# Five one-input VectorE operations of an image stage, written with a tile of ones as second input

## The reference

```python
def _layernorm(x, axis=-1, eps=1e-05):
    m = jnp.mean(x, axis=axis, keepdims=True)
    v = jnp.var(x, axis=axis, keepdims=True)
    return (x - m) / jnp.sqrt(v + eps)
...
        sig = jax.nn.sigmoid(logits)
        choice = sig + e_bias[None, :]
...
        topk_idx = jax.lax.top_k(scores_for_choice, K)[1]
        topk_w = jnp.take_along_axis(sig, topk_idx, axis=1)
        topk_w = topk_w / (topk_w.sum(-1, keepdims=True) + 1e-20)
        topk_w = topk_w * SCALE
```

## Time and profile before

| what | value |
|---|---|
| median of 3 runs | 4340.14 us (4337.72 to 4344.22) |
| span of the profiled execution | 4339.1 us; its page gives no time of its own beside the span |
| instructions | 74496 |
| TensorE matmul, weight load | 3835.0 us (88%), 2899.2 us (67%) |
| VectorE | 3261.9 us (75%), 5523 instructions |
| ScalarE | 2637.8 us (61%), 4838 instructions |
| GpSimd | 3020.4 us (70%), 1609 instructions |
| mean granted TensorE clock | 0.968 of full speed |

### The profile page before, as it was taken

The page is one execution under the profiler, slowest core; times in us unless marked ns, Lnnn a source line. Parts: engine busy times, 40 slices in busy tenths (PEclk is TensorE's granted clock), DMA queues, the critical chain, the costliest instruction groups (busy, mean ns, idle before and its releaser), DMA issues. The chain is left out here.

```text
span 4339.1 us, 74496 instructions
## 1 busy us (share of the span) xinstructions
PE 3835.0 (88%) x22114; PEld 2899.2 (67%) x22114; DVE 3261.9 (75%) x5523; ACT 2637.8 (61%) x4838; POOL 3020.4 (70%) x1609
## 2 busy tenths in 40 slices
PE   3469999999999999999999999988879999999997
PEld 2346666666676666766666666656558888888886
DVE  1788888888889888898888988887246666666663
ACT  1468877888778888788887788875522222222221
POOL 0888888878788787887888878886025555555554
PEclk8669999999999999999999999999989999999999
DMA  3333333333333333333333333321057777777775
GB/s 81 86 85 82 93 90 91 99 83 89 94 84 92 92 84 94 88 94 96 82 90 94 92 89 92 89 71 53 16 127 183 186 184 185 184 183 185 184 186 115
DMA packets 243533, 473.54 MB, mean 109 GB/s; under 512 B 39644, under 2 KB 162080, under 8 KB 243220
## 3 DMA queue, kind: packets, MB, share of 16 engines
q1 hardware_dynamic: 203792, 429.90, 37.4%
q0 software_dynamic: 36864, 37.98, 5.6%
q10 hardware_dynamic: 2564, 1.82, 0.2%
HBM read 404.99 MB, written 64.56 MB: 108 GB/s over the span
## 5 line engine op out<-in xcount | busy, mean ns | idle before, releaser
L507 POOL TENSOR_TENSOR y<-y,state 128x972 f32<-128x972 f32 x448 | 1016.8, 2270 | 336.0 <-DVE state L668 325.3
L486 POOL TENSOR_TENSOR state<-du,b_rows 128x972 f32<-128x972 f32 x512 | 1187.7, 2333 | 3.0
L662 DVE TENSOR_TENSOR_SCAN ps<-ps,state 128x972 f32<-128x972 f32 x512 | 1113.6, 2181 | 61.1 <-ACT ps L530 47.6
L530 ACT ACTIVATE ps<-delta,a_neg 128x324 f32<-128x324 f32 x1536 | 727.3, 521 | 313.0 <-DVE state L668 250.8
L1040 POOL DMA_INDIRECT out_rows<-yo,scatter_idx x256 | 369.5, 1443 | 426.9 <-DMA out_rows<-yo,scatter_idx 354.0
L668 DVE TENSOR_TENSOR state<-ps,c_rows 128x972 f32<-128x972 f32 x512 | 597.7, 1168 | 35.2 <-DVE ps L662 0.5
L782 PE MATMUL ps<-ws_d,inter 116*98 116x192 f32 (+1 forms) x3072 | 539.2, 329 | 16.3 <-issue 12.9
L782 PEld LDWEIGHTS ps<-ws_d,inter 116*98 116x98 f32 (+1 forms) x3072 | 501.7, 175 | 24.2 <-issue 16.3
L1171 PE MATMUL e_ps<-w_down,e_inter 116*96 116x192 f32 x2048 | 359.9, 329 | 102.1 <-DVE yo L1121 102.1
L754 DVE TENSOR_TENSOR inter<-ag,ps 116x648 f32<-116x648 f32 x256 | 211.5, 826 | 316.9 <-PE ps L767 316.9
L1102 DVE TENSOR_TENSOR e_inter<-e_ag,e_ps 116x384 f32<-116x384 f32 x256 | 139.9, 555 | 375.1 <-ACT e_ag L1066 366.6
(11 more groups left out here) (174 smaller groups left out, 7333.4 us busy)
## 6 DMA issues: line engine op xcount, KB each, us to landing
b_rows<-bc_rows SPq DMA_DIRECT2D x256, 324.0 KB, 5.0
c_rows<-bc_rows SPq DMA_DIRECT2D x256, 324.0 KB, 5.7
w_lo<-in_we_up SPq DMA_DIRECT2D x128, 348.0 KB
w_down<-in_we_down SPq DMA_DIRECT2D x128, 348.0 KB
x_in<-in_x SPq DMA_DIRECT2D x32, 1176.0 KB, 7.7
w_hi<-in_we_up SPq DMA_DIRECT2D x256, 116.0 KB
image_cnt<-running_counts SPq DMA_DIRECT2D x256, 81.0 KB
w_lo<-in_we_up SPq DMA_DIRECT2D x128, 116.0 KB
```

The lines of the kernel that those rows point to most:

```text
L486: nc.gpsimd.tensor_tensor(b.state[n % 4][:], b.du[t.p][:], row, ALU.mult).then_inc(input_ready, 1)
L507: nc.gpsimd.tensor_tensor(y, y, b.state[n % 4][:], ALU.add).then_inc(y_added, 1)
L530: ins = nc.scalar.activation(to[:, c * L:c * L + L], b.delta[t.p][:, c, :], ACT.Exp, scale=b.a_neg[:, c, k:k + 1])
L662: nc.vector.tensor_tensor_scan(s, s, b.state[k % 4][:].rearrange("p a t -> p (a t)"), 0.0, ALU.mult, ALU.add).then_inc(scan_done, 1)
```

## The change

Five `tensor_scalar` calls, each with one tensor input, become `scalar_tensor_tensor` calls. The scalar and its operation stay the first step; the second step is a multiplication by a slice of `ones`. Nothing else is added or moved; semaphores and chains stay.

```diff
@@ ln1_stats, ln2_stats
-                        nc.vector.tensor_scalar(stat[:, m + 1, 4, :], b.mean_var[m][:, :, 1], EPS, None, ALU.add).then_inc(ln_var[m], 1)
+                        nc.vector.scalar_tensor_tensor(stat[:, m + 1, 4, :], b.mean_var[m][:, :, 1], EPS, b.ones[:, 0:6], ALU.add, ALU.mult).then_inc(ln_var[m], 1)
@@ choose
-                            nc.vector.tensor_scalar(b.mask[:], b.ch[:], BIG / 2, None, ALU.is_ge).then_inc(mask_ready, 1)
+                            nc.vector.scalar_tensor_tensor(b.mask[:], b.ch[:], BIG / 2, b.ones[:].unsqueeze(1).broadcast_to([128, 6, E]), ALU.is_ge, ALU.mult).then_inc(mask_ready, 1)
@@ weigh
-                            link(nc.vector.tensor_scalar(den, den, 2e-20, None, ALU.add))
+                            link(nc.vector.scalar_tensor_tensor(den, den, 2e-20, b.ones[:, 0:6], ALU.add, ALU.mult))
                             link(nc.vector.reciprocal(b.top8[:, :, 1], den))
-                            nc.vector.tensor_scalar(b.x2[:, :, :, D], b.top8[:, :, 1].rearrange("p (b k) -> p b k", b=2), SCALE, None, ALU.mult).then_inc(factor_ready, 1)
+                            nc.vector.scalar_tensor_tensor(b.x2[:, :, :, D], b.top8[:, :, 1].rearrange("p (b k) -> p b k", b=2), SCALE, b.ones[:, 0:6].rearrange("p (b k) -> p b k", b=2), ALU.mult, ALU.mult).then_inc(factor_ready, 1)
```

## The result

The changed kernel takes 4,351.7 us (median of 8 runs, 4,344.5 to 4,354.4), the kernel before 4,338.9 (8 runs, 4,335.1 to 4,344.2): a ratio of 1.0023, 95% interval 1.0013 to 1.0033. The medians lie 12.8 us apart, and the interval runs from 5.6 to 14.3 us. It is a small loss, of the forecast's size.

The account below looks back on a forecast made before the run. VectorE's run at the head of a body, reaching TensorE through ScalarE, was taken as the bound. Small instructions 0 plus masks 30 x 0.39 = 11.7 us, on a median of 4,340.1, gave 4,351.8 us; range 4,341 to 4,362.

Parts of the forecast that it names:

- The bound: Head of a body: VectorE's long run reaches TensorE through ScalarE, so a delay there is paid about one to one.
- The small instructions, 0 us: L705, L738, L740, 128 instructions: two-input form held by GpSimd to the same end as before, so 0 us.
- The sign that L705 should keep a mean near 750 ns: L705 after the change: mean stays near 750 ns, since its holds by GpSimd stay.
- The mask, 0.39 us: L728, 768 values per partition: one value per cycle in place of two, 0.39 us longer, held or unheld.
- Passed on one to one, 30 times, 11.7 us: 30 of 32 masks stand where VectorE's run has no gap: each 0.39 us reaches the body, 11.7 us.
- the half-absorbed case: Bodies waiting only at L808: TensorE's own work absorbs the delay there, 5.9 us more, 4,346 us; chance 0.22.
- Nothing is left to absorb: Body at 1557.49: TensorE is already 0.07 us late at L808, so any further VectorE delay counts.
- The last two masks: The two unheld L728 of 560 ns, where VectorE idles behind them: taken to cost 0.
- the delays of the two engines are one: At L728: VectorE's 0.39 us and GpSimd's being kept about 0.39 us longer do not add.
- The freed holds, 22 us: Rival: L705, L738, L740 no longer held by GpSimd; TensorE soon bounds, 22 us saved, 4,318 us; chance 0.06.
- The two races at L717: Rivals at L717 against GpSimd: wins where it loses, 4,325 us, chance 0.06; loses where it wins, 4,383 us, chance 0.04.

Follow-up runs that it names:

- the delay behind the mask: Kernel before plus a VectorE sum over 3 x 102 ones right behind L728, about 0.39 us: ratio 1.0042, 14 to 18 us slower.
- the two runs with a pure delay: Kernel before plus one extra VectorE sum, in one run ahead of L728 (ratio 1.0026), in the other behind it (ratio 1.0042).
- the small ones alone: Kernel before with only L705, L738 and L740 given the second input, the mask L728 left one-input: ratio 0.9995.

## Why the prediction was right, point by point

*The bound.* Right: VectorE's run at the head of a body reaches TensorE through ScalarE. Making it longer by 0.38 us lengthened bodies of both kinds by as much (the delay behind the mask), making it shorter took the waits at L795 and L808 away, and with them gone the mask's extra work was free. One thing is to be added: in the long bodies it is not the wait at L808 that sets the length. Five of them, at a clock of 0.98, have only the 0.46 us there of a load that is not late, and last as long as the others; what all 12 have is the wait at L795.

*The small instructions, 0 us.* Right: 0.9995 alone, and pairs of bodies that agree to 0.01 us. But for one row of 5.05 us, the form that the change brings is held to the same point as the old one. That it would be was readable in a few early rows. The sign that L705 should keep a mean near 750 ns was wrong: it was 855. With the old form beside the new mask it is 807 already; where the rest comes from was not separated.

*The mask, 0.39 us.* 0.40 measured, held and unheld, and it is the whole loss.

*Passed on one to one, 30 times, 11.7 us.* Medians 12.8 apart, bodies 0.39 and 0.42 longer. The interval from 5.6 us on would by itself just let the half-absorbed case stand (5.9 us); the pairs of bodies, 0.78 us longer for two masks of 0.40, rule it out. "Nothing is left to absorb" in the short bodies held: L808's load waits 0.30 us more. The last two masks cost nothing, as forecast: the body of the first of them lasts 76.38 us before and 76.37 after. That the total came out within 0.1 us of the forecast's 4,351.8 is luck: with eight runs the kernel before is 1.2 us lower than with three, and the loss 1.1 us larger than my sum. That the delays of the two engines are one was shown by the run that had only VectorE's.

*The freed holds, 22 us.* This price was too low: without the holds the kernel was 45 us faster. I had allowed half a microsecond for short bodies and one for long ones; the 26 bodies of the loop lost 1.2 us in the mean (91.39 to 90.17), 32 us in all. The unrolled bodies, which I had not counted apart, lost 16 us, and the first body began 3.7 us later. Two thirds of those 16 go with the clock: in the first body (0.89 in place of 0.85) and the last long one (0.98 in place of 0.90) TensorE is busy 10.6 us less for the same number of matmuls. Why the clock rose there was not looked into. The chance of that rival was fairly small and the forecast did not rest on it.

*The two races at L717.* I argued that both instructions follow from the same ones, so that no delay could part them, and gave 0.06 and 0.04. Both happen, in single bodies. L717 loses where it won in the two runs with a pure delay. It wins where it lost in three of the 13 bodies that open a turn of the loop in the changed kernel's profile (two at about 1.2 us; the third, 2.49 us, is a win in part) and in three with the small ones alone; the profile of before has none. One of them:

```profile
1283.00 0.82 DVE L754 TENSOR_TENSOR inter<-ag,ps 116x648 f32<-116x648 f32 x1
1285.36 0.96 DVE L717 SCALAR_TENSOR_TENSOR ch<-gt,e_bias 128x768 f32<-128x768 f32 x1 [1.54 <-issue]
```

```profile
1283.25 2.24 POOL L507 TENSOR_TENSOR y<-y,state 128x972 f32<-128x972 f32 x1 [0.98 <-DVE state L668]
1285.45 7.73 POOL L486 TENSOR_TENSOR state<-du,b_rows 128x972 f32<-128x972 f32 x3
```

(VectorE, then GpSimd, in the kernel with the small ones alone.) GpSimd's sum at 1283.25 waited 0.98 us for VectorE's last product, which I had left out as a cause. Then its next instruction begins after L717. That body is 2.0 us shorter, the one before it 1.1 longer. So I had the price wrong too: a won race saves not 2.1 us but some 0.9 (182.09 against 182.95 us for this pair of bodies, 182.8 against 183.7 in the changed kernel), and one pair alone, with the small ones, saved 2.1. It happens in single turns of the loop, not in all, so it makes scatter of a few microseconds and no trend.

## What to carry to other kernels

Before an instruction is given another form to escape a hold, look in the same trace for that form under the same neighbour: two rows of 2.15 us were worth more here than a mechanism. The price of extra work is the extra work times the share of loop bodies in which its run ends last; the same 0.40 us cost 12 us in one kernel, some 4 in another (where the intervals overlap and the bodies carry the reading) and nothing that could be measured in a third. An inserted delay measures a price only if it moves no instruction across the edge of a neighbour's hold.

## What the runs showed of the hardware

A `tensor_scalar` with its one tensor in SBUF and six values lasts 1.5 to 1.9 us (the medians of L738 and L740) while GpSimd works on 128 x 972 values, a `scalar_tensor_tensor` with both in SBUF the same, and `tensor_reduce` and `reciprocal` 0.17 to 0.19 us. On this the Trainium skill, "SBUF — State Buffer", Who interferes with whom, states that a `tensor_scalar`, which can enter a two-port mode, then contends with GpSimd, that an instruction with two SBUF inputs contends with a GpSimd instruction that reads SBUF, and that `tensor_reduce` never does on this chip; the runs agree in all three. What I had not expected is how sharp the edge is: the same mask took 0.55 us in most bodies and 2.65 us in four, and at 649.94 and 743.65, one of each, it starts within 0.01 us of GpSimd's next instruction. And an instruction that loses can lose again: one L705 was held 5.05 us, through three of GpSimd's.

The granted clock of TensorE was 0.85 in one first body and 0.88 in another, 0.90 and 0.96 in the last long one, and those two bodies alone moved one execution by 6 us, half of the effect under study. A body at 0.98 cost nothing in the kernel before and 1.5 us in the one without the small holds (89.2 against 90.7 us in the mean).
